# Two routed expert layers: more places for weights and rows, one-hots of lanes pair by pair, tokens in DRAM by partition

## What is computed

```python
def _L0_ffn_ref(x_btd, Wr, br, W1, b1, W2, b2):
    probs = jax.nn.softmax(x @ Wr + br, axis=-1)
    gates, ids = jax.lax.top_k(probs, K)          # E = 8, K = 2
    ...
    valid = rank < cap                            # cap = ceil(1.2 * N / E)
    ...
    h = jax.nn.silu(jnp.einsum('ecd,edh->ech', xg, W1) + b1[:, None, :])
    out = jnp.einsum('ech,ehd->ecd', h, W2) + b2[:, None, :]
    gated = out * disp_g.reshape(E, cap, 1)
    y = jnp.zeros((N, Dm), x.dtype).at[disp_tok].add(gated.reshape(E * cap, Dm))

def _L1_ffn_ref(x, router_w, w1, w2):
    top_w, top_i = jax.lax.top_k(probs, TOP_K)
    top_w = top_w / jnp.sum(top_w, axis=-1, keepdims=True)
    ...
    h = jax.nn.gelu(jnp.einsum('nc,ech->enh', xf, w1), approximate=False)
    y = jnp.einsum('enh,ehc->enc', h, w2)
    out = jnp.einsum('ne,enc->nc', comb, y)
```

## Time and profile before

| what | us |
|---|---|
| median of 3 runs (1294.24 to 1309.07) | 1296.83 |
| the profiled execution | 1294.54 |
| its span in the trace | 1292.7 |
| PE busy | 1131.5 (88%) |
| DVE busy | 891.1 (69%) |
| ACT busy | 794.4 (61%) |
| POOL busy | 317.5 (25%) |

### The profile page before, as it was taken

The page is one execution under the profiler, slowest core; times in us unless marked ns, Lnnn a source line. Parts: engine busy times, 40 slices in busy tenths (PEclk is TensorE's granted clock), DMA queues, the critical chain, the costliest instruction groups (busy, mean ns, idle before and its releaser), DMA issues.

```text
span 1292.7 us, 21070 instructions
## 1 busy us (share of the span) xinstructions
PE 1131.5 (88%) x7700; PEld 540.5 (42%) x7700; DVE 891.1 (69%) x1564; ACT 794.4 (61%) x1174; POOL 317.5 (25%) x311
## 2 busy tenths in 40 slices
PE   7656777887986999999999999999999999678885
PEld 5322226787853123333333333333333321367875
DVE  3599975572058898888988888888888870352223
ACT  3743322465453048888888889888888889331222
POOL 0088850477526000000000000000000000105772
PEclk8879998898988569999999999999999999788998
DMA  2056502486543300011100111101111000025885
GB/s 98 17 182 215 180 16 74 135 255 197 171 144 103 106 25 18 20 35 36 36 23 14 36 36 35 31 8 34 36 35 31 2 4 3 3 66 166 260 258 176
DMA packets 60023, 107.26 MB, mean 83 GB/s; under 512 B 10273, under 2 KB 24737, under 8 KB 59537
## 3 DMA queue, kind: packets, MB, share of 16 engines
q1 hardware_dynamic: 54576, 94.32, 23.2%
q0 software_dynamic: 4992, 10.23, 3.0%
q10 hardware_dynamic: 352, 1.38, 0.3%
HBM read 92.52 MB, written 13.07 MB: 82 GB/s over the span
## 4 chain that ended last, share of the span: by engine, by line
PE 57%; DVE 11%; issue 9%; DMA 8%; ACT 7%; POOL 6%; SPq 1%; ACTq 0%; DVEq 0%; POOLq 0%
PE psum L846 16%; PE psum L837 15%; PE psum L824 12%; ACT probs L1179 5%; DMA x_got<-xtok_dram,get_row 4%; POOL y_dram L1419 3%; POOL x_got L1412 2%; PE psum L685 2%; PE psum L950 2%; PE psum L663 2%; PE psum L961 1%; DVE ssm_h L1563 1%; PE psum L676 1%; DVE first_max L1848 1%; PE psum L940 1%
## 5 line engine op out<-in xcount | busy, mean ns | idle before, releaser
L1179 ACT ACTIVATE probs<-psum 128x1024 f32<-128x1024 f32 x512 | 496.0, 1024 | 49.8 <-PE psum L837 49.5
L1848 DVE TENSOR_REDUCE tile_max<-psum 128x1 f32<-128x512 f32 x720 | 466.7, 686 | 67.1 <-PE psum L824 61.5
L824 PE MATMUL psum<-k_stack,q_stack 64*128 64x512 bf16 x1014 | 354.0, 396 | 4.1 <-DVE tile_max L1848 1.9
L837 PE MATMUL psum<-q_stack,k_stack 64*128 64x512 bf16 x1024 | 283.7, 380 | 4.3 <-ACT probs L1179 1.2
L846 PE MATMUL psum<-probs,v_head 128*32 128x512 f32 x2048 | 272.7, 605 | 0.6 <-ACT probs L1179 0.6
L824 PEld LDWEIGHTS psum<-k_stack,q_stack 64*128 64x128 bf16 x1014 | 92.0, 94 | 285.4 <-DVE tile_max L1848 122.6
L1386 POOL TENSOR_TENSOR max_parts<-row_max,no_shift 128x8 bf16<-128x8 f32 x32 | 6.4, 200 | 624.9 <-DVE row_max L1833 624.9
L837 PE MATMUL psum<-q_stack,k_ext 64*128 64x512 bf16 x512 | 144.3, 378 | 0.0
L837 PE MATMUL psum<-q_stack,ln_xc 64*128 64x512 bf16 x512 | 136.8, 376 | 0.0
L1171 ACT ACTIVATE ln_xn<-psum 128x512 f32<-128x512 f32 x120 | 71.6, 597 | 76.5 <-PE psum L824 66.8
L1412 POOL DMA_INDIRECT x_got<-xtok_dram,get_row x78 | 79.2, 1016 | 110.2 <-issue 61.7
(11 more groups left out here) (272 smaller groups left out, 1283.6 us busy)
## 6 DMA issues: line engine op xcount, KB each, us to landing
w1r<-w SPq DMA_DIRECT2D x78, 256.0 KB
w2r<-w SPq DMA_DIRECT2D x78, 256.0 KB
ssm_b<-bc_dram SPq DMA_DIRECT2D x32, 512.0 KB, 4.3
k_stack<-k_dram SPq DMA_DIRECT2D x60, 120.0 KB
y_in<-y_dram SPq DMA_DIRECT2D x16, 256.0 KB, 4.8
q_stack<-q_dram SPq DMA_DIRECT2D x32, 96.0 KB
bc_p<-bc_dram SPq DMA_DIRECT2D x5, 512.0 KB, 5.6
k_stack<-k_dram SPq DMA_DIRECT2D x30, 80.0 KB
```

The source lines that it names most:

```text
L824: mm(bank, q_stack[side_rows(side), u, 0, at:at + 128], k_stack[side_rows(side), u, keys:keys + C], start=True, stop=True).then_inc(s1_ps, 1)
L837: return mm(psum[:, 2 * slot + side, :], k[side_rows(side), kt * 128:(kt + 1) * 128], q_stack[side_rows(side), u, part, at:at + C], start= ...
L1179: f(probs[:, kt % 4, hf * HALF:(hf + 1) * HALF], banks(2 * slot, 2), ACT.Exp, scale=SCALE).then_inc(p_ready, 1)
L1848: v.tensor_reduce(top, bank, AX.X, ALU.max).then_inc(s1_read, 1)
```

## The change

In the block loop, `W_RING` goes from 4 to 6, `XG_RING` from 6 to 8 and `OT_RING` from 4 to 6. w1 and w2 get semaphores of their own: w1's place is free again after the `up` of the block six before (`hidden_ps`), w2's after its `down` (`rows_ps`), and `up` waits for w1 alone, `down` for w2.

In the routing, the expert list moves from its place before the slots to behind the one-hots. `lane_hot` is now made by 32 instructions, one per pair column, each comparing the 128 lane numbers with that column's lane (`lane_f`, a column operand); PE waits before each owner matmul for that column's one-hot, and DVE raises `place_ready` at each. `block_hot` and both `block_val` now come before the one-hots, and both values are products with a tensor. The owner values are counted otherwise, so that four steps give `put_row` and `get_row`.

The rows in DRAM change their order: token 128 t + p lies at row 16 p + t of `xtok_dram` and of both halves of `y_dram`, so that a partition's four rows of a chunk are 2 KB in a run.

Some semaphores outside the expert parts are joined (`mod_ready` into `mod_step`, `expA_ready` and `negA_ready` into `rate_step`), with the same waits.

```diff
-W_RING = 4
-XG_RING = 6
+W_RING = 6
+XG_RING = 8
 COL_RING = 3
-OT_RING = 4
+OT_RING = 6
...
-PLACED = [{"either": 3, "experts": 4, "hot": 7}, {"either": 8, "experts": 9, "hot": 12}]
...
+    either = 3 + layer * (PAIRS + 3)
+    return {"either": either, "block": either + 1, "lane": either + 2, "experts": either + PAIRS + 2}
...
-                    sp.dma_start(xtok_dram[c * C:(c + 1) * C].rearrange("(t p) d -> p t d", p=128),
-                                 x_tok[:, c * TPC:(c + 1) * TPC, :]).then_inc(tok_stored, 16)
-                sp.wait_ge(place_ready, PLACED[layer]["experts"])
+                    tiles = slice(c * TPC, (c + 1) * TPC)
+                    sp.dma_start(xtok_dram.rearrange("(p t) d -> p t d", p=128)[:, tiles, :], x_tok[:, tiles, :]).then_inc(tok_stored, 16)
+                sp.wait_ge(place_ready, placed(layer)["experts"])
...
                     if n >= W_RING:
+                        sp.wait_ge(hidden_ps, n - W_RING + 1)
+                    sp.dma_start(w1r[:, k, :], w1_all[bass.ds(e, 1)].rearrange("o p f -> (o p) f")).then_inc(w1_in[k], 16)
+                    if n >= W_RING:
                         sp.wait_ge(rows_ps, n - W_RING + 1)
-                    sp.dma_start(w1r[:, k, :], w1_in[bass.ds(e, 1)].rearrange("o p f -> (o p) f")).then_inc(w_in[k], 16)
-                    sp.dma_start(w2r[:, k, :, :], w2_in[bass.ds(e, 1)].rearrange("o p c d -> (o p) c d")).then_inc(w_in[k], 16)
+                    sp.dma_start(w2r[:, k, :, :], w2_all[bass.ds(e, 1)].rearrange("o p c d -> (o p) c d")).then_inc(w2_in[k], 16)
...
-                        rows = y_dram[n * L + c * C:n * L + (c + 1) * C].rearrange("(t p) d -> p t d", p=128)
-                        sp.dma_start(y_in[:, n, c * TPC:(c + 1) * TPC, :], rows).then_inc(chunk_in[c], 16)
+                        tiles = slice(c * TPC, (c + 1) * TPC)
+                        rows = y_dram[n * L:(n + 1) * L].rearrange("(p t) d -> p t d", p=128)
+                        sp.dma_start(y_in[:, n, tiles, :], rows[:, tiles, :]).then_inc(chunk_in[c], 16)
...
-                pe.wait_ge(place_ready, PLACED[layer]["hot"])
+                pe.wait_ge(place_ready, placed(layer)["block"])
                 for q in range(PAIRS):
-                    i = mm(psum[:, 7, 0:2 * BLOCKS], lane_hot[:, :, q], block_val[:, :, :, q].rearrange("p n b -> p (n b)"),
+                    pe.wait_ge(place_ready, placed(layer)["lane"] + q)
+                    i = mm(psum[:, 7, 0:2 * BLOCKS], lane_hot[:, q, :], block_val[:, :, :, q].rearrange("p n b -> p (n b)"),
                            start=q == 0, stop=q == PAIRS - 1)
...
-                    pe.wait_ge(w_in[k], 32 * (n // W_RING + 1))
+                    pe.wait_ge(w1_in[k], 16 * (n // W_RING + 1))
...
+                    pe.wait_ge(w2_in[k], 16 * (n // W_RING + 1))
                     pe.wait_ge(hidden_ready, n + 1)
...
-                v.tensor_scalar(tile_expert_i[:], tile_expert[:], float(NE - 1), None, ALU.min).then_inc(place_ready, 1)
...
-                v.tensor_tensor(lane_hot[:], lane_b[:].unsqueeze(1).to_broadcast([128, 128, PAIRS]), lane_wide[:],
-                                ALU.is_equal).then_inc(place_ready, 1)
                 step(v.tensor_tensor(block_hot[:], block_b[:].unsqueeze(1).to_broadcast([128, BLOCKS, PAIRS]), block_wide[:],
                                      ALU.is_equal))
-                v.tensor_scalar(block_val[:, 0], block_hot[:], placing("token"), None, ALU.mult).then_inc(place_ready, 1)
-                v.tensor_tensor(block_val[:, 1], block_hot[:], pair_no[:].unsqueeze(1).to_broadcast([128, BLOCKS, PAIRS]),
-                                ALU.mult).then_inc(place_ready, 1)
+                for n, values in enumerate((pair_row, pair_tile)):
+                    i = v.tensor_tensor(block_val[:, n], block_hot[:], values[:].unsqueeze(1).to_broadcast([128, BLOCKS, PAIRS]), ALU.mult)
+                i.then_inc(place_ready, 1)
+                step(v.tensor_copy(lane_f[:], lane_i[:]))
+                for q in range(PAIRS):
+                    v.tensor_scalar(lane_hot[:, q, :], lanes[:], lane_f[:, q:q + 1], None, ALU.is_equal).then_inc(place_ready, 1)
...
+                v.tensor_scalar(tile_expert_i[:], tile_expert[:], float(NE - 1), None, ALU.min).then_inc(place_ready, 1)
...
-                step(v.tensor_copy(put_row[:], row_f[:]))
+                step(v.scalar_tensor_tensor(vacant[:], row, 0.0, placing("spare"), ALU.is_equal, ALU.mult))
+                step(v.scalar_tensor_tensor(row_f[:], row, -float(TILES), vacant[:], ALU.add, ALU.add))
+                step(v.tensor_tensor(put_row[:], row_f[:], tile, ALU.add))
```

More of the change, by code:

```diff
@@ L70 @@
 PAIRS = 2 * TILES
-W_RING = 4
-XG_RING = 6
+W_RING = 6
+XG_RING = 8
 COL_RING = 3
-OT_RING = 4
+OT_RING = 6
 GATES_TURNED = 30
-PLACE = ["earlier", "lane", "step", "block", "pair", "no_reset", "token", "spare", "expert", "first", "b1"]
-PLACE_SIZE = {"earlier": 128, "lane": 128, "step": TILES, "block": BLOCKS, "pair": PAIRS, "no_reset": TILES * NE, "token": 1,
+PLACE = ["earlier", "lane", "step", "block", "pair", "no_reset", "row", "spare", "expert", "first", "b1"]
+PLACE_SIZE = {"earlier": 128, "lane": 128, "step": TILES, "block": BLOCKS, "pair": PAIRS, "no_reset": TILES * NE, "row": PAIRS,
               "spare": BLOCKS, "expert": NE, "first": NE, "b1": HC * NE}
@@ L99, with placed @@
 STACK_LOADS = 14
-PLACED = [{"either": 3, "experts": 4, "hot": 7}, {"either": 8, "experts": 9, "hot": 12}]
-WIDES = [3, 9]
-PADS = 6
+def placed(layer):
+    either = 3 + layer * (PAIRS + 3)
+    return {"either": either, "block": either + 1, "lane": either + 2, "experts": either + PAIRS + 2}
+WIDES = [4, 11]
+PADS = 7
 def maxima_order():
@@ L453, in build @@
         tok_ps, tok_copied, tok_stored = sem("tok_ps"), sem("tok_copied"), sem("tok_stored")
-        w_in = [sem(f"w_in{k}") for k in range(W_RING)]
+        w1_in = [sem(f"w1_in{k}") for k in range(W_RING)]
+        w2_in = [sem(f"w2_in{k}") for k in range(W_RING)]
         got = [sem(f"got{k}") for k in range(XG_RING)]
@@ L1053, in scaled @@
                     if n == 0:
-                        act.wait_ge(mod_ready, 2)
+                        act.wait_ge(mod_step, MOD_STEPS)
                     act.wait_ge(ln_xn_ready, n + 1)
@@ L1085, in ssm_scan @@
             def ssm_scan():
-                act.wait_ge(negA_ready, 1)
+                act.wait_ge(rate_step, 2)
                 act.wait_ge(dt_x_ready, 2)
@@ L1685, in place @@
                 dve.wait_ge(count_ps, 3 * layer + 3)
-                token, pair = (psum[:, 7, n * BLOCKS:(n + 1) * BLOCKS] for n in range(2))
-                step(v.tensor_scalar(vacant[:], token, 0.0, None, ALU.is_equal))
-                step(v.tensor_scalar(owner[:], token, -1.0, None, ALU.add))
-                step(v.scalar_tensor_tensor(owner[:], pair, 128.0, owner[:], ALU.mult, ALU.add))
-                step(v.tensor_tensor(row_f[:], vacant[:], placing("spare"), ALU.mult))
-                step(v.tensor_tensor(row_f[:], row_f[:], owner[:], ALU.add))
-                step(v.tensor_copy(put_row[:], row_f[:]))
+                row, tile = (psum[:, 7, n * BLOCKS:(n + 1) * BLOCKS] for n in range(2))
+                step(v.scalar_tensor_tensor(vacant[:], row, 0.0, placing("spare"), ALU.is_equal, ALU.mult))
+                step(v.scalar_tensor_tensor(row_f[:], row, -float(TILES), vacant[:], ALU.add, ALU.add))
+                step(v.tensor_tensor(put_row[:], row_f[:], tile, ALU.add))
                 v.tensor_scalar(get_row[:], put_row[:], L - 1, None, ALU.bitwise_and).then_inc(rows_ready, 1)
```

45 lines of the change are left out of this document (22 added, 23 removed).

## The result

| | before | after |
|---|---|---|
| median of 20 runs, us (lowest to highest) | 1302.95 (1290.96 to 1313.79) | 1291.59 (1278.85 to 1301.92) |
| ratio after/before, 95% interval | | 0.9901 [0.9874, 0.9929] |
| profiled execution, us; span | 1294.54; 1292.7 | 1295.05; 1293.2 |

The changed kernel is 1.0% faster, some 13 us (9 to 16), where 1281 us was forecast (1273 to 1290) for a gain of 15.5. The ratio compares fast runs alone, which is why it says 13 us while the two medians, over all runs, are 11.4 apart. Of the 10.6 us between forecast and measured median 6.1 are the base: in twenty runs the kernel before has a median of 1302.95, not 1296.83, the median of three. By the medians the gain itself is 4.1 short of 15.5.

The account below looks back on a forecast made before the run. POOL was taken to set the block loop's pace at 2.57 us, DMA engines close behind. Gains of 6.5 + 5.2 + 2 x 1.9 = 15.5 us gave 1281.3 from the median shown, forecast as 1281 us, range 1273 to 1290.

Parts of the forecast that it names:

- 6.5, 5.2 and 1.9 a layer: Forecast gains in us: layer 0's expert part 6.5, layer 1's 5.2, and the read-back 1.9 in each layer.
- Places, middle and end of the loop: Block loops: two more gathers ahead save two 2.57 us pairs in layer 1; layer 0 gains 6.5 us.
- One-hots: Routing on DVE: 32 small steps at 0.165 us each, 5.3 us in all, beside PE's owner matmuls.
- Gain: 2 x 2.57 = 5.1, if the first send stays where it is ... at 1180.4: Layer 1's loop: two fewer pairs gain 5.1 us; the first send follows the eight gathers, at 1180.4.
- the first turn come some 0.2 later: Layer 0's start: the later gate copy delays the first turn 0.2 us; first send from 246.97 to 247.2.
- PE's turning of the gates: Layer 0's start: PE's step waiting for the gate copy, forecast to start at 232.1.
- I take 1.9 a layer: Read-back at each layer's end: 2 KB instead of 512 B runs gain 1.9 us a layer (ends 0 and 3).
- rival 2: Read-back: the 2 KB reads gain nothing, 3.8 us less gain, 1285.1 us; chance 0.14.
- Rival 5: Block loop: rows 8 KB apart in DRAM slow gathers and scatters, pace 3.05, 1311 us; chance 0.05.
- Freed apart: Block loop's weight places: freeing w1 after the up and w2 after the down products gains 0.
- The expert list's move: Routing on DVE: moving the expert list behind the one-hots takes 1.13 us off the front.
- rival 3: Places fall short: PE in layer 0 waits (+1.6), weights delay first rows (+1 a layer), 1284.9 us; chance 0.09.

Follow-up runs that it names:

- xg8_only: Changed kernel with weight and outgoing-row places back at 4, gathered-row places kept at 8; expert parts 293.2 us together, against 294.2 in the changed kernel.
- before_xg8: The kernel before with only XG_RING raised from 6 to 8; ratio to the kernel before 0.9925 in ten runs.
- after_warm: Changed kernel with more filler matmuls in layer 1: 15 instead of 10 before the first turned block, 3 behind it; ratio to the kernel before 0.9888.
- list_front: Changed kernel with the expert list back at the front of the routing, so weights are asked for sooner; expert parts 292.8 us together, against 294.2.
- rows_old: Changed kernel with both DRAM arrays in the old row order, read back in 512 B runs; ratio to the kernel before 0.9856 in four runs.
- rows_old_5: Same kernel as rows_old (changed kernel, old DRAM row order), measured in twelve runs; ratio to the kernel before 0.9909.
- rings_old: Changed kernel with places back at 4 for weights, 6 for gathered rows, 4 for outgoing rows; ratio to the kernel before 0.995 in ten runs.
- read_near: Changed kernel reading each read-back chunk where its 2 KB runs lie end to end (wrong tokens' rows); expert parts 291.9 us together, 2.3 less.
- pool_gates: Changed kernel with layer 0's gates turned ahead of the owner matmuls and the expert list made by POOL; ratio to the kernel before 0.9864.

## Why the prediction was right and wrong

The measured median lies outside the range. The largest part of that is the base, 6.1 us: three runs of a kernel whose twenty lie between 1291 and 1314. Off the base of twenty runs the same sum gives 1287.5, inside the range, so by the number alone the forecast was unlucky; but the gain was too large as well, and that is where steps failed. Counted from the logits, against forecasts of 6.5, 5.2 and 1.9 a layer:

- **Places, middle and end of the loop: right.** The loop of layer 1 lost 5.1 us from first to last send (forecast 2 x 2.57 = 5.1), that of layer 0 lost 6.5. The way was right too: two pairs fewer, eight gathers and eight sends in a row, pace 2.57, PE as the later one in layer 0's tail (forecast 21.5 from the gates' second turning to the last send, measured 21.2). That xg8_only does the same in both layers, and before_xg8 in layer 1, says the gathered rows' places are the cause. For layer 0's tail I had credited part to further weight places; xg8_only does without them.
- **One-hots: right.** 0.165 each, complete beside PE. "VectorE: DVE Perf Modes" of the Trainium skill, in its TRN2 errata section, warned of small tiles; the measured 0.165 us lies between the two estimates worked out from its figures (0.094 and 0.190), so the trace agrees that each small step pays a fixed cost, and 32 of them still fit beside PE. That the value met the forecast to the third digit is partly luck: its ends were 0.033 and 0.28.
- **The step that failed first: "Gain: 2 x 2.57 = 5.1, if the first send stays where it is ... at 1180.4".** It did not stay: 33.8 instead of 32.5 behind the logits, 1.3 late. I had summed POOL's gathers and put nothing for the landing and PE's first products. The change makes rows arrive later (weights now travel beside them: 4.2 us from gather to turn instead of 3.5), the ten fillers no longer reach to them, PE idles twice for 1 us, and the clock from there on is 0.69. after_warm shows that link: 0.7 of the 1.3 come back with 8 more fillers. list_front shows the rest: without weights beside the first rows the first send follows right behind the gathers.
- **The same step in layer 0: "the first turn come some 0.2 later".** It came 1.4 later (32.3 against 30.9), and the first send at 38.7 where I had 37.4: 1.3 late. The gate copy was where I put it; what was mis-sized is "PE's turning of the gates", taken at 4.76. It took 5.87, at a granted clock of 0.64 (0.78 in the kernel before). In all eight profiles with the changed routing and the gates turned in this place it took 5.24 to 6.60; in rows_old, rows_old_5 and rings_old it took 6.4 to 6.6, the fillers behind it 3.9 to 4.0 instead of 2.32, and the first turn came at 34.5 to 34.6. PE now idles 2.60 ahead of it, but that idling is not shown to be the cause: in list_front the gap is 1.49 and the turning takes 5.86. So the term was sized at a higher clock than it got, and what holds the clock down there stays open.
- **"I take 1.9 a layer" for reads in 2 KB runs: wrong.** 0 was measured (rival 2's value), but not for rival 2's reason. "DMA: Bandwidth & Descriptors", Specifications, of the Trainium skill has 512 B as enough for line rate; no run here reads 512 B runs end to end, so none tests that. What the runs show is the distance: read_near reads the same 2 MB in the same runs of 2 KB 1.3 us sooner when they lie end to end. I took slices of weight reads, where the runs lie end to end, as the price of reads 8 KB apart. Rival 5 named that distance, for the gathers and scatters, where it did nothing; it acts on the reads.
- **Freed apart: 0 was forecast, and no run takes it alone.** xg8_only against before_xg8 leaves room for some of it in layer 0. The expert list's move: I counted 1.13 of DVE's front, and 0.5 (layer 1) and 0 (layer 0) are its whole effect, less the clock it costs through the later weights.
- **Sum.** 15.5 - 1.3 - 1.3 - 3.8 = 9.1; the expert parts show 8.5, since what follows the last send took 0.2 and 0.3 longer in the two layers. The repeated runs say 12.8 (9.3 to 16.4). What lies between stays open: the untouched stretch varies by 18 us from profile to profile, and single profiles cannot say whether the changed kernel is a little quicker there.

Crowding at the start, rival 3, was right in kind for layer 1, with 1 us as its price, but 0.7 of the 1.3 us went through PE's clock, which the rival did not have. In layer 0 the first turn has no wait for rows; what was late there was the gates' turning.

## What to carry to other kernels

When a change takes work off the engine ahead of PE, follow PE through the gap that opens: a microsecond or two of idling just before a dependent chain can nearly halve the speed of its first products (1.82 to 1.92 us for 1.06 here) and eat half of what was saved (2.0 of 4.4 us in layer 0 of pool_gates); filler has to reach up to the arrival of the data, and its count must be set anew after each such change. The depth of the gather ring decided this loop because a gather and a send share one queue: each further block gathered ahead takes a pair off the paced part, and one constant gave most of the gain. A transfer's price is read from a row with the same run length and the same distance between runs.

## What the runs showed of the hardware

- A granted clock that falls behind short waits: idling of 1.03 and 0.98 us around the first rows went with 0.69 over 5.6 us; only 0.34 there, and filler between, with 1.00; 2.80 us with 0.56. The idling alone does not tell: in layer 1 of rows_old it was 0.34 and 0.71 us, and the clock, low since the wait for the owner matmuls, was 0.60 over those 5.6 us. These are averages of a stretch at the two levels of 1.2 and 2.4 GHz: a block's eight up products take 1.06 us at the upper one, and 1.82 to 1.92 where it was mostly the lower. "TensorE: Matmul & The Clock Gate" of the Trainium skill describes, under HAM oscillation, a kernel whose PE falls to the lower level at each wait for a transfer; these rows agree in kind, but with waits of about 1 us, shorter than those it describes.
- 2 MB read from DRAM in 2 KB runs: 9.7 us from issue to ACT's end with the runs end to end (read_near, both layers), 10.9 to 11.0 in the changed kernel with 8 KB between their starts, 11.1 to 11.5 in 512 B runs with 64 KB between a partition's (rows_old, rows_old_5). The last two do not differ beyond what single profiles do; the first does.
- A tensor_scalar on 128 bf16 columns with a column operand: one every 0.165 us when none waits for another, although one alone, in float32, shows 0.28.
